# Run ends by 0/1 products with the destination table, a plain float32 product inside the scan, and no hold in its first round

## What is computed

```python
def _L0_gnn_ref(x, edge_index, w1, b1, g1, bt1, wg, bg, gg, btg, w2, b2, g2, bt2):
    h = batch_norm(x @ w1.T + b1, g1, bt1)          # x is 6250 x 256
    src, dst = (edge_index[0], edge_index[1])       # 200000 edges, dst is sorted
    diff = h[src] - h[dst]
    m = jax.ops.segment_max(diff, dst, num_segments=N)
    m = jnp.where(jnp.isfinite(m), m, 0.0)
    hg = jnp.concatenate([h, m], axis=-1)
    hg = jax.nn.gelu(batch_norm(hg @ wg.T + bg, gg, btg))
    return batch_norm(hg @ w2.T + b2, g2, bt2) + res
x = x + _L0_gnn_ref(_layernorm(x), stack([src, dst]), ...)
x = x + _L0_ffn_ref(_layernorm(x)[None], ...)[0]    # 8 experts, 3 layers each, softmax mix
```

## Time and profile before

| what | value |
|---|---|
| median of three runs | 3529.28 us (3520.81 to 3536.49) |
| the profiled execution | 3531.34 us, of it 3529.6 us in the span |
| busy in the span: POOL / DVE / PE / ACT | 1632.1 / 1811.5 / 1400.1 / 733.2 us |
| head block | 0 to 97 us |
| scan block | 97 to 2420 us |
| first gather / last gather / last chain step | 97.6 / 2335.5 / 2342.2 us |
| granted clock of PE in nearly all of the scan | 0.50 |

### The profile page before, as it was taken

How to read it: one execution, slowest core, us unless ns; L and a number is a source line. 1 busy time by engine, 2 the same in 40 slices (tenths; PEclk the granted TensorE clock), 3 DMA queues, 4 the chain that set the end, 5 groups by cost and what they waited for, 6 DMA issues and landing times. The chain is left out here.

```text
span 3529.6 us, 25757 instructions
## 1 busy us (share of the span) xinstructions
PE 1400.1 (40%) x8911; PEld 1223.8 (35%) x8911; DVE 1811.5 (51%) x3414; ACT 733.2 (21%) x852; POOL 1632.1 (46%) x1658
## 2 busy tenths in 40 slices
PE   6200000000010010000010011247889999999998
PEld 6200000000000000000000000246779999999998
DVE  6563465445345355345345345322966555555544
ACT  5100000000000000000000000133356556555554
POOL 1576776767767676766667667533210000000000
PEclk9555555555555555555555555568989999999999
DMA  7375565656556555556556456531132433442231
GB/s 233 111 240 173 198 235 190 212 191 221 189 183 231 175 193 199 175 177 207 163 173 219 160 186 204 168 116 59 31 107 90 139 111 118 128 132 103 105 118 64
DMA packets 166245, 567.27 MB, mean 161 GB/s; under 512 B 32710, under 2 KB 69766, under 8 KB 158948
## 3 DMA queue, kind: packets, MB, share of 16 engines
q1 hardware_dynamic: 82740, 346.77, 26.7%
q0 software_dynamic: 83376, 218.87, 21.7%
HBM read 328.58 MB, written 236.93 MB: 160 GB/s over the span
## 5 line engine op out<-in xcount | busy, mean ns | idle before, releaser
L627 POOL DMA_INDIRECT ring<-runs,src_i x1564 | 1547.4, 989 | 763.5 <-issue 454.1
L722 DVE SCALAR_TENSOR_TENSOR ring<-ring,pen 128x256 f32<-128x256 f32 x1564 | 757.5, 484 | 848.2 <-remote 315.2
L864 PE MATMUL ps<-oh_hi,oh_lo 128*128 128x49 bf16 x1575 | 160.9, 214 | 1903.5 <-issue 1302.0
L864 PEld LDWEIGHTS ps<-oh_hi,oh_lo 128*128 128x128 bf16 x1575 | 98.6, 113 | 1965.8 <-issue 1345.2
L731 DVE TENSOR_TENSOR oh_lo<-lo,ps 128x896 bf16<-128x896 bf16 x224 | 242.1, 1081 | 224.3 <-remote 200.4
L1422 ACT ACTIVATE av<-ps,vecs 128x896 f32<-128x896 f32 x224 | 246.2, 1099 | 329.5 <-PE ps L186 329.5
L649 ACT ACTIVATE zs<-ps 128x512 fp32r<-128x512 f32 (+1 forms) x56 | 27.4, 541 | 1177.0 <-remote 1166.3
L1570 DVE TENSOR_TENSOR h2l<-av,h2h 128x896 fp32r<-128x896 f32 x112 | 122.3, 1092 | 203.1 <-ACT h2h L1424 203.1
L1768 PE MATMUL ps<-fw,h2h 128*128 128x256 f32 x784 | 225.1, 287 | 3.3 <-DVE h2l L1570 3.3
L1577 DVE SCALAR_TENSOR_TENSOR y<-ps,wv,y 128x256 f32<-128x256 f32 x392 | 168.8, 478 | 111.2 <-PE ps L1770 110.5
L1769 PE MATMUL ps<-fw,h2l 128*128 128x256 f32 x784 | 222.5, 284 | 0.0
(11 more groups left out here) (274 smaller groups left out, 2865.6 us busy)
## 6 DMA issues: line engine op xcount, KB each, us to landing
runs<-ring SPq DMA_DIRECT2D x136, 896.0 KB
fw<-wsp SPq DMA_DIRECT2D x56, 1536.0 KB, 6.4
runs<-ring SPq DMA_DIRECT2D x102, 768.0 KB
ring<-runs,src_i POOLq DMA_INDIRECT x1564
res_d<-x_all SPq DMA_DIRECT2D x7, 896.0 KB
y<-res_d SPq DMA_DIRECT2D x7, 896.0 KB, 6.9
part<-in_Wx SPq DMA_DIRECT2D x16, 384.0 KB
wsp<-part_hi SPq DMA_DIRECT2D x16, 384.0 KB
```

Of the source, the lines that this page charges most:

```text
L627: pool.indirect_dma_start(ring[:, k, :], None, runs[0:N, :], bass.IndirectOffsetOnAxis(ap=src_i[:, STEPS * i + k:STEPS * i + k + 1], axis= ...
L722: dve.scalar_tensor_tensor(out=ring[:, k, :], in0=ring[:, before, :], scalar=pen[:, STEPS * i + k:STEPS * i + k + 1], in1=ring[:, k, :], o ...
L864: r = pe.matmul(ps[:, 0, 0:NT], oh_lo[t % NSET][:, n, :], oh_hi[t % NSET][:, n, :], start=False, stop=False, skip_group_check=True)
```

## The change

1. **Head.** `digits` goes. `table` puts the destinations as float32 into `tab` (128 windows x 4 pieces of Q = 391, and one more column with the window's own number), and counts the first run (as `digits(2)` did). POOL issues one more small DMA for `next_i`, the first destination of the following window, and no longer makes `tri` and `zr`.
2. **Run ends.** The histogram goes. For each of the 49 blocks of 128 nodes, DVE makes `sel` (a 128 x 128 matrix of 0 and 1: which window holds the end of this node's run, `choose`), PE multiplies it with the four pieces of `tab` in plain float32 (`window`), so that each node's partition holds its window's 1564 destinations in PSUM, and DVE counts there those that are at most the node, and those that equal it (`count`). A slot of this work stands at every 29th chain step, and `count(t)` stands one slot behind `choose(t)`.
3. **z on its side.** PE turns z once, ACT copies it into `zt` in SBUF, where it stays, and DVE takes the statistics from `zt`. `z_hi`, `z_lo`, `row_low` and the second turning go.
4. **The late product** is one plain float32 product instead of three fp32r ones, with weights `was` (scaled by ACT). Its 14 pieces are issued by PE inside rounds 2 to 16, each behind a `window`; ACT evicts a piece behind its part of a weight split. The loads of `war` and `wbq` stand ahead of the rounds on SP, `bgx` is made in round 1.
5. **Hold.** POOL's wait on s_ch within round 0 goes. In later rounds it stays.

```diff
-                            if (k - GO[g]) % 4 == 0 and STEPS * i + k > LEAD:
+                            if i and (k - GO[g]) % 4 == 0:
                                 pool.wait_ge(s_ch, STEPS * i + k - LEAD)
...
+                def choose(t):
+                    dve.tensor_scalar(sel[:], iof[:], w_from[:, t:t + 1], None, ALU.is_ge)
+                    dve.drain()
+                    dve.scalar_tensor_tensor(out=sel[:], in0=iof[:], scalar=w_upto[:, t:t + 1], in1=sel[:],
+                                             op0=ALU.is_lt, op1=ALU.mult).then_inc(s_sel, 1)
+
+                def count(t):
+                    dve.wait_ge(s_win, t + 1)
+                    dve.tensor_scalar(junk[:], ps[:, 0:4, 0:Q], nodef[:, t:t + 1], None, ALU.is_le, ALU.add, accum_out=cnt[:, 0, t:t + 1])
+                    dve.drain()
+                    dve.tensor_scalar(junk[:], ps[:, 0:4, 0:Q], nodef[:, t:t + 1], None, ALU.is_equal, ALU.add, accum_out=cnt[:, 1, t:t + 1])
+                    dve.tensor_copy(cnt[:, 2, t:t + 1], ps[:, 3, Q:Q + 1])
...
                     for g in range(NG):
-                        k = GO[g]
-                        if first:
-                            row_low(g)
-                        for j in range(4):
-                            chain(i, k + j)
-                        low_hots(i, g)
-                        chain(i, k + 4)
-                        high_hots(i, g)
-                        for k in range(GO[g] + 5, GO[g + 1]):
+                        for k in range(GO[g], GO[g + 1]):
                             chain(i, k)
+                            j, at = divmod(STEPS * i + k - SLOT0, SLOTW)
+                            if at == 0 and 0 <= j <= NT:
+                                if j:
+                                    count(j - 1)
+                                if j < NT:
+                                    choose(j)
...
-                for t in range(NG * HR + 1):
-                    counts(t)
...
+                def window(t):
+                    pe.wait_ge(s_sel, t + 1)
+                    for b in range(4):
+                        r = pe.matmul(ps[:, b, 0:Q + 1], sel[:], tab[:, b, :], start=True, stop=True)
+                    r.then_inc(s_win, 1)
...
+                def sums(n):
                     c, a, w = piece_of(n)
+                    if n:
+                        pe.wait_ge(s_aev, n)
+                    for m in range(GM):
+                        for k in range(KC):
+                            r = pe.matmul(ps[:, 4 + m, 0:w], was[:, k, m * P:(m + 1) * P], zt[:, c, 0, k, a:a + w], start=k == 0, stop=k == KC - 1)
+                    r.then_inc(s_A, 1)
...
+                done = 0
+                for t in range(NT):
+                    window(t)
+                    if done < NPIECE and SLOT0 + SLOTW * t >= STEPS * (done + 2):
+                        if done == 0:
+                            pe.wait_ge(s_was, 1)
+                        sums(done)
+                        done += 1
```

More of the change, by code:

```diff
@@ L526, in _ @@
                         penalties()
-                    elif c < 4:
-                        digits(c - 1)
+                    elif c == 1:
+                        table()
             @block.tensor
@@ L852, in _ @@
                 dve.sem_inc(s_c4, 1)
-                for k in range(GO[3], STEPS):
+                for k in range(GO[1], STEPS):
                     chain(PG, k)
@@ L918, in _ @@
-                pe.matmul(ps[:, 0, 128:128 + NT], ones[:], cnt[:, 0, :], start=True, stop=True).then_inc(s_c3, 1)
-                pe.wait_ge(s_wal, 1)
-                pe.wait_ge(s_tev, 2 * KC)
-                for n in range(NPIECE):
-                    if n == 6:
-                        pe.wait_ge(s_c4, 1)
-                        pe.matmul(ps[:, 0, 256:256 + 2 * P], ones[0:1, :], rowf[0:1, :], start=True, stop=True)
-                    for m in range(GM):
-                        sums(n, m)
-                        if m % 2 and n + 2 < NPIECE:
-                            columns(n + 2, m // 2)
+                done = 0
@@ L930, in build @@
+                for t in range(NT):
[5 more added lines that the diff above has]
+                        done += 1
+                pe.wait_ge(s_c4, 1)
+                pe.matmul(ps[:, 0, 256:256 + 2 * P], ones[0:1, :], rowf[0:1, :], start=True, stop=True)
         s_fg, s_fx = sem("s_fg"), sem("s_fx")
```

280 lines of the change are left out of this document (95 added, 185 removed).

## The result

The changed kernel takes 3441.34 us (median of 4 runs, 3436.25 to 3445.14), the kernel before 3532.28 us (4 runs). The ratio is 0.9747, with a 95% interval of 0.9719 to 0.9774: 91 us faster, where 154 were forecast. The time lies above the range (3255 to 3425).

A forecast was written before the change was run, and what follows sets the result against it. POOL's gathers were taken to pace the scan, followed by 78 us of late product on PE. Terms -74 - 21 - 20 - 59 + 20 = -154 us from 3531.3 gave 3377, as a median 3375 us; range 3255 to 3425.

The forecast's parts named there:

- End of the scan, -74: After the last chain step: the late product moves into the scan under PE's idle time, gaining 74 us (71 to 77).
- Round 0, -20: Start of the scan: without POOL's hold the 47th gather starts at 160 instead of 180 us, gaining 20 us (0 to 25).
- a round 0 that still ends near 180 us: Sign of a wrong forecast: the 47th gather was to start at about 160 us.
- The wait before 2259, -21: DVE's wait before round 33 for PE's work behind the histogram goes, gaining 21 us (15 to 22).
- PE's slow stretches, -69 with 10 kept: In the scan, PE's late, single instructions fall from eight stretches to about three: 10 of 69 us stay, gain 59 (30 to 69).
- More than ten: Sign of a wrong forecast: more than ten slow stretches on DVE, where about eight were expected.
- The +20: DVE's slow stretches in the scan: longer counts add 20 us (from 124 less to 80 more); the eight stretches stay.
- Head, 0: Before the scan: digits and table lie beside PE's and ACT's work, one small DMA more; 0, within 2 us.
- B: Rival: slots on DVE cost more than they seem, windows and weight splits come late; 3420 us (3410 to 3450), chance 0.19.
- C: Rival: PE can't deliver windows in time, count waits and POOL stalls; slower than before, about 3560 us, chance 0.03.
- D: Rival: the late product isn't hidden in the scan after all; 3450 us, chance 0.03.
- A: Rival: DVE's slow stretches go too, as PE's instruction traffic falls to 40%; 3230 us, chance 0.15.

The follow-up runs named there:

- g1_before: The kernel before, unmodified, profiled in a set without slow stretches: 3232.65 us.
- g2_before_late: The kernel before with PE starting the fourth of 14 late-product pieces only after the last chain step: 3302.46 us against 3234.84, ratio 1.0217.
- h1_hold: The changed kernel with POOL's hold in round 0 put back, in a set with slow stretches: 3424.22 us, 0.9694 of the kernel before.
- i3_before_nohold: The kernel before with only POOL's hold in round 0 taken out, in a set with slow stretches: 3551.87 us, ratio 1.0054.
- f1_after: The changed kernel, unmodified, in a set without slow stretches: 3227.96 us, 0.9976 of the kernel before.
- g5_window_late: The changed kernel with PE holding each window back until the last chain step ahead of its count: 3460.93 us, 0.9792 of the kernel before.
- e1_hold: The changed kernel with POOL's hold in round 0 put back, in a set without slow stretches: 3224.41 us, 0.9969 of the kernel before.
- f2_hold: The changed kernel with POOL's hold in round 0 kept, second set without slow stretches: 3227.87 us, 0.9976 of the kernel before.
- i1_noslots: The changed kernel without choose, window and count (counts set to zero, output wrong), with slow stretches: 3430.42 us, 0.9706 of the kernel before.
- h2_pause: The changed kernel with the hold and POOL waiting every third round until its gathers landed, with slow stretches: 3426.28 us, 0.9684 of the kernel before.

## Why the prediction was wrong, point by point

**End of the scan, -74: right in size (-73.6).** "The late product leaves the end" held, and the block behind the scan starts 3.7 us after the last chain step; I took 4. What I didn't ask is why the product was at the end. It fits beside the last two rounds (g1_before), and late copies of ACT out of PSUM had pushed it out (g2_before_late makes the same tail by a delay on PE, +68 us). So this gain, too, exists only with slow stretches.

**Round 0, -20: wrong in sign (+7), the largest error.** The step that failed is "Statistics run from SBUF behind ACT's copy; I leave their end where it is, since PE sets it in both". PE sets it in neither. It had each piece ready long before (33 us in the changed kernel, for the 18th) and waited for room; the end is set by the engine that reads the pieces, DVE before and ACT now, and that engine was late until 5 to 8 us after POOL's gathers paused, in all eight traces that have slow stretches. So the hold, which I priced as a pure wait, brings the statistics' end forward: without it they end 27 to 30 us later, and the 47th gather comes at 190 us and not at 160. Kept, the hold is worth 15 to 17 us (h1_hold) and in the kernel before 17 us (i3_before_nohold). Why a pause of POOL ends the lateness is open. A smaller fault: step 25 and its store were put 16 us behind the first chain step, while 18.6 us lie between that step and the 47th gather. The prediction's own sign of being wrong, a round 0 that still ends near 180 us, was met: it ends at 190.

**The wait before 2259, -21: less than half (-8.6).** I had the wrong engine: DVE waited in the end for ACT, which came 38 us late, and not for PE's work. That wait is gone, but the small instructions that remain ("2 us") fell into a slow stretch of DVE (two of them 6.5 and 7.0 us late) and cost a wait of 13.8 us. In h1_hold, where no stretch lies on them, the last two rounds take 117 us (gathers 2177.5 to 2294.1) instead of 138.6, and the whole 21 us come; 6 of them are lost again behind the last gather, where a stretch does lie. Whether one falls there is chance.

**PE's slow stretches, -69 with 10 kept: too large.** Three were forecast, none came: PE begins each of the 49 windows within 2 us of its `sel`. The mis-sized term is the 69: I took the first of seven stretches for all. Against g1_before, rounds 1 to 31 of the kernel before lose 178 us, not the 193 of my sum (124 for DVE, 69 for PE). Against f1_after, those of the changed kernel lose 155; 124 + 20 + 10 = 154 were forecast. The total of what stays was right, but partly by luck: it is all DVE's, with nothing of PE's. What was there came out 15 us too high.

**DVE.** About eight stretches were forecast, eleven came, and longer ones: some 1340 us in all, from the first to the last late instruction of each, against some 950 in the eight of the kernel before (late: more than 0.6 us idle with nothing to wait for). More than ten was a sign of being wrong. The +20 were put on counts that last longer than the gap; in fact the two instructions behind a drain come late, 82 + 85 us, part of which POOL's lead hides. Reason wrong; the size, at most 31 us (155 - 124), is near the 20.

**Head, 0: +3.2**, outside the 2 us that I allowed. Part of it is scatter: in the fifteen traces that have the changed head the first gather starts at 97.4 to 102.1 us, in five of the kernel before at 96.9 to 98.0. The cause wasn't tried.

**Rivals.** B gave 3430 (3410 to 3450) and holds the time, by other means: not late windows and split weights but round 0. C did not come: PE's windows were never late, and even windows held back by hand cost 16 to 20 us (g5_window_late). D did not come: no product is left behind the scan. A's time, 3231, is what the changed kernel takes without slow stretches (3228), but by another way, since the kernel before loses them as well. That is what no case held: the loss belongs to the run. Cut at the same events, the kernel before loses to slow stretches 15.8 us in round 0, 178.2 in rounds 1 to 31, 20.5 in rounds 32 and 33 and 73.8 at the end (the differences of its two tables above), and of just these four terms my sum was made. Where they are zero, the change is worth 0.24%.

**What stays open:** why instructions come late in some runs and not in others. The first three sets had none of it, the last two had it, as did the first executions, and the chips of the second and fourth set bear the same number, though that doesn't make them one device. Also open is what begins and ends a stretch of DVE, and why ACT's and DVE's late reading at the start ends with POOL's pause.

**The best version** is the changed kernel with the hold kept (e1_hold, f2_hold, h1_hold): 0.9694 of the kernel before with slow stretches, 0.9969 and 0.9976 without. It beats the changed kernel by 15 to 17 us where there are slow stretches and is within the measurement of it elsewhere.

## What to carry to other kernels

Idle time that the profile puts down to nothing ("issue", with instructions 1 to 10 us apart) may be a wait after all: look for an instruction of another engine that ended just before the idle time did, and at how long the data had been ready. It may also belong to the run and not to the kernel: before forecasting what a change saves of it, look at the kernel in other runs, and give the forecast for both. A tail in which one engine works alone asks for two causes, the work and why it started late. And a hold on one engine may be what ends the lateness of another: measure its removal alone.

## What the runs showed of the hardware

- The same program took 3532 to 3535 us in some sets of runs and 3235 to 3237 in others (medians), with nothing in between, and with the same granted clock (0.50 in rounds 1 to 31 of both). The difference is idle time with nothing to wait for, on DVE, PE and ACT.
- The instruction queue has the same 70 packets and 1.15 MB in g1_before, where no such idle time is seen. The Trainium skill, Runtime: NRT & Kernel Launch, section Instruction fetch mechanics, says that refills are mostly hidden: g1_before and f1_after agree, the first profiles don't, if it is refills that they wait for; no run here shows that.
- In a slow stretch a chain step comes each 1.40 us (i1_noslots), and an instruction behind a drain 2 to 4 us late (h1_hold at 838.90 and 940.40).
- The late reading of the turned z, by ACT or DVE, ended 5.0 to 8.2 us after POOL's last gather, eight times out of eight. At the end of the scan of the kernel before the same shows: ACT's copies followed each other at once from 2343.8 us on, 8.3 us after the last gather. Stops of POOL of 2 us (h2_pause) and 8.8 us (h1_hold) did not end a slow stretch of DVE in the rounds.
- Elementwise work of DVE from float32 to bf16 beside gathers made a gather's issue on POOL 1.52 us long instead of 0.95 (medians).
- A plain float32 product of 392 columns shows as two loads and two products of 814 ns on average, so a window of four takes 4.3 to 5.6 us: between the 3.3 and 6.7 of the forecast's bounds.

```profile
L813 PE MATMUL ps<-tab,sel 128*128 128x392 f32 x392 | 250.3, 814 | 1641.8 <-DVE sel L701 1076.0 <-issue 565.8
```
